# A fused decoder layer on one core: where v's gate, the copies of late weights and x1's turn stand

## The reference, cut to what matters

```
x1 = layernorm(x + attn(x))             # linear attention: (q k^T) v without a softmax, 8 heads of 64
x2 = layernorm(x1 + xattn(x1, ctx))     # 16 heads of 32, 154 keys, key mask, softmax
xr = mu_r*x2 + (1-mu_r)*x2_prev         # x2_prev: the row before
xk = mu_k*x2 + (1-mu_k)*x2_prev
y  = layernorm(x2 + sigmoid(xr W_r) * (relu(xk W_k)^2 W_v))
```

## Time and profile before

| | |
|---|---|
| median of 3 runs | 917.88 us (916.47 to 919.17) |
| profiled execution | 916.23 us, span 914.2 us |
| PE busy | 880.3 us (96%) |
| DVE busy | 717.1 us (78%) |
| ACT busy | 534.0 us (58%) |
| POOL busy | 503.2 us (55%) |
| mean granted clock of PE | 0.996 |

### The profile page before, as it was taken

How to read it: one execution, slowest core, us unless ns; L and a number is a source line. 1 busy time by engine, 2 the same in 40 slices (tenths; PEclk the granted TensorE clock), 3 DMA queues, 4 the chain that set the end, 5 groups by cost and what they waited for, 6 DMA issues and landing times.

```text
span 914.2 us, 23136 instructions
## 1 busy us (share of the span) xinstructions
PE 880.3 (96%) x8566; PEld 729.8 (80%) x8566; DVE 717.1 (78%) x2050; ACT 534.0 (58%) x1628; POOL 503.2 (55%) x505
## 2 busy tenths in 40 slices
PE   8999999999899999999999999998999999999997
PEld 7867767788688888888877878787878788888886
DVE  7687566677897878787888878787878788888675
ACT  7456326758465756565746465656565656565631
POOL 1035015667666565656565657575756657575520
PEclk9999999999999999999999999999999999999998
DMA  9792020104313131313322222223131313130001
GB/s 306 232 266 64 23 95 2 43 3 165 97 32 112 36 109 39 106 41 102 104 78 56 85 54 82 66 67 82 59 90 48 99 48 100 48 94 25 2 24 46
DMA packets 82252, 73.80 MB, mean 81 GB/s; under 512 B 7134, under 2 KB 66526, under 8 KB 82014
## 3 DMA queue, kind: packets, MB, share of 16 engines
q1 hardware_dynamic: 78542, 65.27, 23.6%
q10 hardware_dynamic: 3600, 7.08, 2.5%
HBM read 47.73 MB, written 23.33 MB: 78 GB/s over the span
## 4 chain that ended last, share of the span: by engine, by line
PE 24%; POOL 21%; DVE 16%; issue 16%; DMA 6%; ACT 3%; SPq 1%; POOLq 0%; DVEq 0%
POOL row_inv L1555 6%; POOL weight L1563 6%; PE dense L94 6%; PE dense L96 5%; PE dense L95 5%; DVE x_squares L1219 3%; POOL xt_lo L1535 3%; DMA xt_raw<-x_scratch 3%; POOL prob_rest L1562 2%; DVE stats L1184 2%; DMA xt_raw<-x_cols 2%; DMA x_scratch<-x_squares 2%; PE turned L1800 2%; POOL rstd L1542 2%; DVE mix_k_raw L1300 2%
## 5 line engine op out<-in xcount | busy, mean ns | idle before, releaser
L1555 POOL TENSOR_TENSOR row_inv<-row_sum,minus_one 128x4 f32<-128x4 f32 x128 | 140.8, 1100 | 179.6 <-ACT prob L887 175.2
L887 ACT ACTIVATE prob<-prob,row_min 128x154 f32<-128x154 f32 x512 | 209.5, 416 | 18.2 <-DVE row_min L1252 18.2
L1563 POOL TENSOR_TENSOR weight<-prob,row_inv 128x512 f32<-128x512 f32 x128 | 142.2, 1111 | 0.0
L1252 DVE CUSTOM_DVE_ANT_0 prob<-scores,mask_add 128x154 f32<-128x154 f32 x512 | 128.5, 312 | 4.1 <-PE scores L1786 3.7
L895 ACT ACTIVATE prob_t<-turned 128x512 f32<-128x512 f32 x128 | 75.4, 589 | 54.3 <-PE turned L1800 54.3
L887 ACT ACTIVATION_READ_ACCUMULATOR prob<-prob,row_min 128x1 f32 x512 | 98.5, 192 | 0.0
L1800 PE MATMUL turned<-ident,weight 128*128 128x128 f32 x512 | 77.0, 273 | 5.7 <-DVE o_t_lo L1259 4.0
L908 ACT ACTIVATE o_t_hi<-turned 128x256 fp32r<-128x256 f32 x64 | 24.2, 379 | 97.0 <-PE turned L1822 97.0
L1800 PEld LDWEIGHTS turned<-ident,weight 128*128 128x128 f32 x512 | 61.1, 140 | 20.5 <-issue 8.4
L94 PE MATMUL dense<-xt_hi,cross_wq_hi 128*128 128x256 f32 x256 | 77.4, 302 | 0.0
L94 PE MATMUL dense<-mix_k_hi,ffn_wk_hi 128*128 128x256 f32 x256 | 75.1, 293 | 0.0
(11 more groups left out here) (283 smaller groups left out, 2640.4 us busy)
## 6 DMA issues: line engine op xcount, KB each, us to landing
x_scratch<-x_squares SPq DMA_DIRECT2D x52, 256.0 KB, 2.6
x_rows<-x_rows SPq DMA_DIRECT2D x32, 256.0 KB, 4.5
xt_raw<-x_cols SPq DMA_DIRECT2D x16, 512.0 KB, 3.8
out<-gate_then_y SPq DMA_DIRECT2D x15, 512.0 KB, 2.8
x_t<-x_scratch SPq DMA_DIRECT2D x104, 64.0 KB, 2.4
xt_raw<-x_scratch SPq DMA_DIRECT2D x52, 128.0 KB, 2.8
mask_in<-mask SPq DMA_DIRECT2D x16, 154.0 KB, 2.4
cross_wv<-cross_wv SPq DMA_DIRECT2D x2, 512.0 KB, 5.0
```

The costliest lines, as they stand in the source:

```text
L887: m = act.activation(keys, keys, ACT.Exp, bias=row_min[:, buf, t, h:h + 1], scale=-1.0, accum_out=row_sum[:, buf, t, h:h + 1])
L1252: m = dve.tensor_tensor_reduce(exp_slot(n, u)[:, i * CTX:(i + 1) * CTX], s_bank[:, h, t * CTX:(t + 1) * CTX], mask_add[n % 2][:, t, :], -S ...
L1555: pool.tensor_tensor(row_inv[:, buf, t, :], row_sum[:, buf, t, :], minus_one[:], ALU.pow).then_inc(*p_inv.up)
L1563: pool.tensor_tensor(first, early, inv_early, ALU.mult).then_inc(*p_norm.up)
```

## The change

Six edits in the orders of the engines. No product and no DMA is added or removed.

- v_finish is cut in two: v_gated (the gate) and v_sums (the sum and the moments). In the loop, v_gated(e, 0) stands ahead of difference(f) and v_sums(e, 0) behind blend(f, "k"); o_low(n, 2) moves ahead of k_mix_low.
- In ACT's loop the queries of the next group (take_q(a, 0)) are copied ahead of the high part of k's mix.
- The high and low parts of the late weights are made in halves, each with its own count on the semaphore. ACT's copy of ffn_wr moves ahead of k_high(e, 0), that of ffn_wv behind o_high(n, 0); DVE's low part of ffn_wr moves ahead of o_finish(f, 1), and k_low(e, 0) behind it in round 2.
- The low parts of the next m: part 2 moves from round 7 to the end of round 6, part 3 ahead of the normalisation of y3.
- POOL's r_mix_low of group 0 moves from the end of round 1 behind x_low(3) in round 2.
- In round 0 PE turns x1 of group 1 ahead of values(0, 1) and makes fold_u(2, 3) behind scores(0, 3). The waits for the banks follow: fold_u(2) and (3) wait for the low parts of x1, x1_turn(1, t) for the copy of u's parts 0 and 1, and q_product(1, 0) for the copy of u's part 3. ACT and DVE take x1's parts earlier to match, and ACT copies u's parts 2 and 3 behind o_high(0, 1).

```diff
 def weight_high(name):
     act.wait_ge(*w_here.at(late.index(name)))
-    act.activation(w[name][0][:], raw[name][:], ACT.Copy).then_inc(*w_hi_ok.up)
+    for ks in halves_of:
+        act.activation(w[name][0][:, ks, :], raw[name][:, ks, :], ACT.Copy).then_inc(*w_hi_ok.up)
...
 # ACT, round 0
-take_u(2, 3)
-o_high(0, 1)
 x1t_high(1, 0)
 x1t_high(1, 1)
+o_high(0, 1)
+take_u(2, 3)
...
 # ACT, loop
+if n == 2:
+    weight_high("ffn_wr")
 k_high(e, 0)
 exponentials(n, 1, 1)
-if n == 2:
-    weight_high("ffn_wr")
-else:
+if n > 2:
     mix_high(e, "r")
 o_high(n, 0)
+if n == 2:
+    weight_high("ffn_wv")
...
+take_q(a, 0)
 mix_high(f, "k")
-take_q(a, 0)
 o_high(n, 2)
...
 # DVE, round 0: behind bias_u(0, 1) instead of behind make_mask
+x1t_low(1, 0)
+x1t_low(1, 1)
...
 # DVE, loop
 k_square(e, 0)
+if a == GPB:
+    next_m_low(3)
 if live(e - 1):
     normalise(3, e - 1, y3)
 o_finish(f, 0)
-k_low(e, 0)
-if a == GPB:
-    next_m_low(2, 3)
+if n == 2:
+    weight_low("ffn_wr")
+else:
+    k_low(e, 0)
 o_finish(f, 1)
 if n == 2:
-    weight_low("ffn_wr")
+    k_low(e, 0)
...
 masked_min(n, 3, 1)
+v_gated(e, 0)
 difference(f)
 blend(f, "k")
-v_finish(e, 0)
+v_sums(e, 0)
+o_low(n, 2)
 k_mix_low(f)
-o_low(n, 2)
 masked_min(a, 0, 0)
 masked_min(a, 0, 1)
...
 if a == GPB - 1:
-    next_m_low(0, 1)
+    next_m_low(0, 1, 2)
...
 # POOL, loop
 x_low(a)
+if e == 0:
+    r_mix_low(e)
 weigh(n, 1, 0)
...
 # PE, round 0
 transposes(0, 1, 1)
-fold_u(2, 3)
+x1_turn(1, 0)
+x1_turn(1, 1)
 values(0, 1)
 scores(0, 3)
-x1_turn(1, 0)
-x1_turn(1, 1)
+fold_u(2, 3)
 transposes(0, 2, 0)
 q_product(1, 0)
```

More of the change, by code:

```diff
@@ L690, in layers @@
         late = ("ffn_wk", "ffn_wr", "ffn_wv")
-        w_here, w_hi_ok, w_lo_ok, bo_here = flag("w_here", 1, 16), flag("w_hi"), flag("w_lo"), flag("bo_here", 1, 16)
+        w_here, w_hi_ok, w_lo_ok, bo_here = flag("w_here", 1, 16), flag("w_hi", 2), flag("w_lo", 2), flag("bo_here", 1, 16)
+        halves_of = (slice(0, KT // 2), slice(KT // 2, KT))
         ft_mm, ft_ok = flag("fold_t_mm", KT - 1), flag("fold_t_ok", KT)
@@ L1041, in act_program @@
                 take_rest(n, 1)
-                if n == 2:
-                    weight_high("ffn_wv")
                 exponentials(n, 2, 1)
@@ L1123, in weight_low @@
             def weight_low(name):
-                dve.wait_ge(*w_hi_ok.at(late.index(name)))
-                dve.tensor_tensor(w[name][1][:], raw[name][:], f32(w[name][0][:]), ALU.subtract).then_inc(*w_lo_ok.up)
+                for i, ks in enumerate(halves_of):
+                    dve.wait_ge(*w_hi_ok.at(late.index(name), i + 1))
+                    dve.tensor_tensor(w[name][1][:, ks, :], raw[name][:, ks, :], f32(w[name][0][:, ks, :]),
+                                      ALU.subtract).then_inc(*w_lo_ok.up)
             def take_t(*parts):
@@ L1319, in k_low, with v_gated @@
                                   ALU.subtract).then_inc(*ka_lo_ok.up)
-            def v_finish(n, t):
+            def v_gated(n, t):
                 dve.wait_ge(*r_out.at(n, t + 1))
@@ L1325, in v_finish, with v_sums @@
                                          ALU.mult).then_inc(*v_out.up)
+            def v_sums(n, t):
                 dve.wait_ge(*v_out.at(n, t + 1))
@@ L1330, in v_finish @@
                 moments(3, n, t, y3)
+            def v_finish(n, t):
+                v_gated(n, t)
+                v_sums(n, t)
             def end_finish(i):
@@ L1402, in dve_program @@
                     add_one(0, 1, 2)
-                x1t_low(a, 0)
-                x1t_low(a, 1)
+                if n:
+                    x1t_low(a, 0)
+                    x1t_low(a, 1)
                 if live(n):
@@ L1612, in pool_program @@
                 weigh(a, 0, 1)
-                if live(f):
-                    r_mix_low(f)
             for n in range(2, LAST):
@@ L1701, in fold_u @@
                     else:
-                        pe.wait_ge(*fu_ok.at(0, c - 1))
+                        pe.wait_ge(*x1t_lo_ok.at(1, c - 1))
                     pe.matmul((d1, d0)[c % 2][:], kv_t1[:, c, :], fold["self_wo"][:, c, :],
@@ L1760, in x1_turn @@
                 elif n == 1:
-                    pe.wait_ge(*fu_ok.at(0, 3 + t))
+                    pe.wait_ge(*fu_ok.at(0, 1 + t))
                 else:
@@ L1768, in q_product @@
                     pe.wait_ge(*(x1_low_at(n) if moved_x1(n) else x1t_lo_ok.at(n)))
-                    if h == 0 and n >= 3:
+                    if h == 0 and n == 1:
+                        pe.wait_ge(*fu_ok.at(0, KT))
+                    elif h == 0 and n >= 3:
                         pe.wait_ge(*r_out.at(n - 3, 2))
```

## The result

The changed kernel took 893.23 us (median of 4 runs, 893.02 to 894.20) against 918.04 us (4 runs, 916.47 to 919.17): the ratio is 0.9733 [0.9716, 0.9750]. Its profiled execution took 894.2 us with a span of 892.2, that is 22.0 us under the span of before; 20.0 had been forecast. Between the medians it is 24.8 us, and 893.23 us lies 4.7 under the forecast of 897.9 and 0.3 under the lower end given for it (893.5).

What follows compares the result with a forecast made beforehand. PE, busy 880.3 of the 914.2 us span, bounds the kernel, so only its waits can go: 14.0 + 1.3 + 3.2 + 1.5 = 20.0 us, profiled 896.2, median 897.9 us; range 893.5 to 908 (8 in 10).

Steps and rivals of the forecast that it cites:

- The gate: Rounds 3 to 14: PE's wait for v's gating goes, 14.3 us plus 1.8 of seams, 16.1 gross, net 14.0 us.
- give-back: Rounds 3 to 14: later row minima make values(n,3) wait, 0.1 or 0.25 us a round, 2.1 us lost in all.
- will still end there, nothing ahead of them becomes shorter: Round 9: DVE's row minima still end at 591.0, so values(n,3) waits; 0.25 us lost in each of six rounds.
- Queries first: ACT copies the queries ahead of k's mix_high: costs nothing, saves about 0.7 us a round that would otherwise come back.
- m's low part: Round 7: PE's 1.2 us wait for m_lo goes, with 0.15 of seam; gain 1.3 us, bounds 0.8 and 1.5.
- Round 2: Weights in halves, r_mix_low behind x_low, with v's 1.2 us: gain 3.2 us, bounds 4.5 and -1.
- the term of 1.4 for o_low(2,1): In round 2 the subtraction starts near 245.3, o_low(2,1) ends before PE wants it, and PE's 1.43 us wait goes.
- Round 0: x1's turn ahead of u's last two products: 0.55 us at q_product(1,0), 1.7 by the clock; ACT passes on 1.5 us.
- Rival 1: DVE meets POOL's weights, minima come 0.8 us later, values(n,3) waits; 9.6 us over twelve rounds, 907.5 us; chance 0.18.
- rival 3: Difference and k_mix_low each collide for 1.6 us in every round: 14.8 us slower, 932.7 us; chance 0.03.
- Rival 2: The opening gives nothing: clock still falls, ACT late with u, halves hold o_finish in round 2; 901.9 us; chance 0.12.
- rival 4: PE's waits turn into others at the same place, such as xt_lo: no change, 917.9 us; chance 0.04.

Runs made afterwards that it cites:

- the two kernels with other orders: The changed kernel with v's first gate ahead of masked_min(n,3,1), 903.18 us, and the changed kernel with all of v_finish(e,0) ahead of the difference, 912.83 us.

## Why the prediction was right

**The gate: right, and its give-back wrong.** Gross 16.1 us was forecast, and the waits went in all twelve rounds; by matched products PE gained 16.3 us at these twelve places (0.8 to 1.3 in rounds 3 to 7, 13 and 14, 1.7 to 2.1 in rounds 8 to 12) and 17.0 in these rounds without m's part. The step that failed is "will still end there, nothing ahead of them becomes shorter", and with it the 2.1 us given back. Round 9 of the changed kernel, ACT and PE, as in the earlier trace rows:

```profile
578.73 0.42 ACT L889 ACTIVATE prob<-prob,row_min 128x154 f32<-128x154 f32 x1 [0.19 <-DVE row_min L1256]
...
580.85 0.36 ACT L902 ACTIVATE prob_t<-turned 128x256 f32<-128x256 f32 x1
...
581.40 0.67 PE L1841 MATMUL turned<-prob_t,v_first 64*32 64x128 f32 x32
```

The exponentials do wait for the minima now, as forecast, but the copies end 0.19 us ahead of PE and not 0.1 behind. What stands ahead became shorter. From the end of the minima ahead of the difference or the gate to the end of the next group's first tile DVE took 9.04 to 9.06 us in rounds 3 to 12 before; in the changed kernel it takes 8.85 to 9.15 in rounds 3 to 6, where it waits for v_product(e,0), and 8.3 to 8.6 in rounds 7 to 11. The operations meet POOL at other moments: k_mix_low 1.22 us where it was 1.44, the blends of k 2.35 where the earlier trace rows have 2.60, against 0.38 for the edge column where it was 0.21: 0.3 us in sum. With k_mix_low put back first, 1.44 came back in ten of twelve rounds, so its place makes its duration. In round 9 the whole stretch takes 8.50 us, 0.55 less than before, of which the durations named are 0.3. The shift also moved time about behind the minima: the blends of r take 2.53 us beside POOL, 1.78 before, and the copy behind them 0.17 where it took 0.89.

**Queries first: right, underpriced.** 0.7 a round holds for rounds 3 to 6 (0.64); rounds 7 to 13 need it more (up to 1.35), 12 us in all.

**m's low part: 0.7 us where 1.3 were forecast.** The wait in round 7 went (1.3 with its seam). Failed is "Part 2 moves into DVE's idle 0.97 us at the end of round 6". DVE there, before and changed, and PE of the changed kernel:

```profile
453.33 0.90 DVE L1277 COPY x_t<-x_t 128x4 f32<-128x4 f32 x1
454.13 1.28 DVE L1176 TENSOR_TENSOR m_lo<-m_raw,m_hi 128x512 fp32r<-128x512 f32 x2
456.38 0.42 DVE L1259 TENSOR_TENSOR o_t_lo<-turned,o_t_hi 128x256 fp32r<-128x256 f32 x1 [0.97 <-ACT o_t_hi L908]
```
```profile
444.76 2.53 DVE L1304 SCALAR_TENSOR_TENSOR mix_r_raw<-mix_r_raw,cols,x_t 128x256 f32<-128x256 f32 x4
447.33 0.17 DVE L1281 COPY x_t<-x_t 128x4 f32<-128x4 f32 x1
447.41 1.89 DVE L1180 TENSOR_TENSOR m_lo<-m_raw,m_hi 128x512 fp32r<-128x512 f32 x3
449.22 0.42 DVE L1263 TENSOR_TENSOR o_t_lo<-turned,o_t_hi 128x256 fp32r<-128x256 f32 x1
```
```profile
449.78 0.63 PE L1819 MATMUL turned<-ident,weight 128*128 128x128 f32 x4 [0.53 <-DVE o_t_lo L1263]
```

o_t_hi had been ready since 448.4. The blends of r are 0.75 us longer (2.53 after 1.78), but the copy behind them is 0.73 shorter, so the two cancel. What used the idle time up is that PE, no longer held by the gate, came forward against DVE: at the end of round 6 o_t_hi is ready 7.9 us earlier than before, and DVE is 6.7 us earlier at its m_lo. So the 0.97 us was gone before part 2 with its 0.6 came. The slack of the old schedule was taken for that of the new one.

**Round 2: 2.7 us where 3.2 were forecast.** x_low's 0.3, the 0.5 of the chain and v's 1.2 came nearly as worked out, and the loss at o_finish too. Short is the term of 1.4 for o_low(2,1). DVE, POOL and PE of the changed kernel, as in the earlier trace rows:

```profile
243.68 2.52 DVE L1128 TENSOR_TENSOR ffn_wv_lo<-ffn_wv_raw,ffn_wv_hi 128x1024 fp32r<-128x1024 f32 x2
246.12 1.16 DVE L1184 TENSOR_SCALAR mask_add<-mask_in 128x308 f32<-128x308 int32 x1
...
245.07 2.02 POOL L1580 TENSOR_TENSOR weight<-prob,row_inv 128x512 f32<-128x512 f32 x1
...
247.75 0.63 PE L1819 MATMUL turned<-ident,weight 128*128 128x128 f32 x4 [0.56 <-DVE o_t_lo L1263]
```

The mask, 0.31 us in the later rounds, takes 1.16 here until POOL's weight, itself 2.02 for 1.04, is done. 0.86 of the 1.43 went. The split of ffn_wr cost its own: 3.53 us for two halves beside POOL's r_mix_low, where the same edit for ffn_wv cost 2.52.

**Round 0: right almost to the row.** 1.56 us against 1.5. PE and ACT of the changed kernel:

```profile
158.08 1.98 PE L1720 MATMUL dense<-self_wo,kv_t 128*128 128x512 f32 x4 [1.07 <-DVE xt_lo L1219]
...
167.87 0.50 PE L1734 MATMUL dense<-u_hi,self_wq_hi 128*128 128x512 f32 x1 [0.36 <-ACT u_hi L851]
...
160.59 0.41 ACT L889 ACTIVATE prob<-prob,row_min 128x154 f32<-128x154 f32 x1
```

158.0, 167.9 and 160.6 had been forecast for these three. Up to here PE wins 1.9 us (2.3 forecast): 0.4 at q_product(1, 0), where 0.55 was forecast, and 1.5 by the clock, where it was 1.7. It then waits 0.36 us for u_hi, so that 1.6 is left. Before, u_hi had come just in time (PE idled 0.03 us), so that ACT took less of the gain than the prediction says. The 1.5 of the clock is there only against an execution in which the clock falls; as the mean clocks of the kernel with the old round 0 show, not every one is such. That part of the forecast is right for the profiled pair, and partly by luck.

**The sum.** By matched products 1.6 + 2.7 + 0.7 + 17.0 = 22.0 us. The sizes missed have both signs (+3.0 for the gate, -0.6 and -0.5 for m and round 2), and the total came out only 2 us better because they partly cancel, which is luck. Against the medians (24.8 us) it is 4.8 short: the forecast carried the 1.65 us between the profiled execution and the median over unchanged, though it goes in part with a clock that the changed kernel hardly loses. The lower end of 893.5 belongs to 24.4 us, with round 2's bound at 4.5; the sum printed beside it (23.9) has 4.0. Rival 1 (called the second where the prediction speaks of a collision of 1 us) and rival 3 needed a longer way of DVE to the minima in every round: only the two kernels with other orders showed it. Rival 2 fell with the clock in round 0, rival 4 with the first row of waits.

## What to carry to other kernels

Where PE waits for a short DVE operation that stands behind longer ones with slack, move that one operation alone ahead, and walk every in-order queue behind it: the sum and statistics moved along cost 19.8 us, more than half of it through a copy on ACT whose data were there and which stood behind another. When PE is brought forward, every other consumer that it asks comes due by as much, so look for the call with the least slack on each engine (here the queries, 12 us) and price it in the rounds that gain most. Read the slack from a schedule shifted by the change, not from the old trace, since PE comes forward against the other engines, and durations on DVE and POOL depend on which of two instructions starts first.

## What the runs showed of the hardware that was not expected

- A wait of the same length at the same place in the program changed the clock in one kernel and not in another. Round 7's wait for o_t_lo, first in the kernel with the whole finish ahead, then in the one with the gate one step earlier; PE, then the stretch behind it (columns of the earlier trace rows, the clock third from the end):

```profile
455.75 0.78 PE L1818 MATMUL turned<-ident,weight 128*128 128x128 f32 x4 [2.19 <-DVE o_t_lo L1263]
...
455.70:464.30 8.60, 8.55 (x36) 7.05 (x37) 6.26 (x25) 5.32 (x21) 4.33 (x4) 0.80 0.17 64
```
```profile
455.26 0.63 PE L1819 MATMUL turned<-ident,weight 128*128 128x128 f32 x4 [2.18 <-DVE o_t_lo L1263]
...
455.20:463.80 8.60, 8.54 (x43) 7.12 (x44) 7.56 (x27) 6.18 (x21) 4.20 (x4) 1.00 0.17 64
```

  After the 2.19 us the clock averaged 0.80, part of it at 1.2 GHz; after the 2.18 us it stayed at 2.4. In the profiled executions it fell in round 0 behind 2.00 us in each of the three kernels that had that wait, and in none that had 1.06 or 1.07 us there, while a wait of 1.95 us in round 12 of the kernel before left it alone. Nor do the executions of one kernel agree: three of four with round 0's old order have a mean clock of 0.999, too high for that fall. The length of one wait doesn't decide it; what else does stays open. The prediction's step (a gap of 1.0 us leaves the clock) held in every profile.
- An exchange of order by one step on DVE changed durations of DVE operations that were not moved by 0.2 to 0.8 us each, through who starts first against POOL.
